# Deformable 3x3 convolution on Trainium2: sets of sampling centres with 6x10 regions, the gather over 64 rows in two partition halves, the spread in fp32, and a convolution that reads the samples in place

## The reference

```python
x1  = x + L0(gn(x))          # gn: mean and variance per image and channel; L0: 16 Fourier modes
                             # along rows and along columns, and a 1x1 mix
out = x1 + L1(gn(x1))

def L1(x):                   # deformable 3x3 convolution, 32 -> 32 channels
    om = conv2d(x, w_om, 3x3, padding 1) + b_om
    off = om[:, :18]; mask = sigmoid(om[:, 18:])
    ys = dy + ky + base_y; xs = dx + kx + base_x         # for each of the nine taps
    vals = bilinear_sample(x, ys, xs) * mask             # zero outside the image
    return einsum('bckhw,ock->bohw', vals, weight) + bias
```

## Time and profile before

| | |
|---|---|
| runs | 2192.13, 2203.97, 2210.58 us; median 2203.97 |
| span of the profiled execution | 2204.3 us |
| PE busy | 1875.0 us, 85% |
| DVE busy | 1707.6 us, 77% |
| ACT busy | 1630.4 us, 74% |
| POOL busy | 1377.4 us, 62% |
| first and last output add (L780) | 337.2 and 2197.6 us |
| DMA, data | 362.74 MB, 58.7% of 16 engines |
| DMA, instructions | 117 packets, 1.92 MB |
| chain of waits that ended last | PE 45%, DVE 16%, "issue" 13% |

### The profile page before, as it was taken

How to read it: one execution, slowest core, us unless ns; L and a number is a source line. 1 busy time by engine, 2 the same in 40 slices (tenths; PEclk the granted TensorE clock), 3 DMA queues, 4 the chain that set the end, 5 groups by cost and what they waited for, 6 DMA issues and landing times.

```text
span 2204.3 us, 126941 instructions
## 1 busy us (share of the span) xinstructions
PE 1875.0 (85%) x50241; PEld 1307.4 (59%) x50241; DVE 1707.6 (77%) x2942; ACT 1630.4 (74%) x2854; POOL 1377.4 (62%) x1803
## 2 busy tenths in 40 slices
PE   8566169988999888898999899999999999999995
PEld 3321046655666555565666666666666666666663
DVE  8689358866888667686888788888888888888883
ACT  0003358877888777787888888888888888888883
POOL 0000057766777666676777777777777777777772
PEclk9699679999999999999999999999999999999997
DMA  9026636655666555655666666666666666666663
GB/s 339 1 114 252 255 104 173 172 142 140 175 172 172 144 143 152 160 151 145 173 172 173 160 169 177 172 172 172 172 172 172 172 175 169 170 171 173 172 165 92
DMA packets 196603, 364.84 MB, mean 166 GB/s; under 512 B 39760, under 2 KB 122480, under 8 KB 192368
## 3 DMA queue, kind: packets, MB, share of 16 engines
q1 hardware_dynamic: 196464, 362.74, 58.7%
HBM read 159.38 MB, written 52.22 MB: 96 GB/s over the span
## 4 chain that ended last, share of the span: by engine, by line
PE 45%; DVE 16%; issue 13%; POOL 4%; SPq 3%; ACT 2%; DVEq 2%; DMA 1%; POOLq 0%; ACTq 0%
PE pV L987 14%; PE pE L966 10%; DVE big L753 9%; PE pM L1012 8%; PE pM L999 7%; PE pR L1026 3%; SPq L421 3%; DVE halves L748 3%; DVE big L734 3%; POOL halves L493 2%; POOL prod L484 2%; PE pM L1033 1%; ACT halves L588 1%; DVE big L761 1%; DMA v<-big 1%
## 5 line engine op out<-in xcount | busy, mean ns | idle before, releaser
L753 DVE COPY big<-pE 128x768 f32<-128x768 f32 x768 | 725.7, 945 | 256.4 <-PE pE L966 246.3
L493 POOL TENSOR_TENSOR halves<-prod,halves 128x300 f16<-128x300 f32 x768 | 604.4, 787 | 429.8 <-DVE halves L748 275.8
L594 ACT ACTIVATE big<-pE 128x768 f32<-128x768 f32 x768 | 634.5, 826 | 112.3 <-PE pE L966 111.5
L987 PE MATMUL pV<-big 128*32 128x144 f32 x16384 | 671.7, 293 | 26.5 <-issue 22.6
L484 POOL TENSOR_TENSOR prod<-big 128x300 f32<-128x300 f32 x768 | 558.7, 728 | 73.3
L966 PE MATMUL pE<-big,sel_s 32*128 32x64 f16 (+1 forms) x24576 | 412.8, 203 | 144.6 <-DVE big L753 98.9
L966 PEld LDWEIGHTS pE<-big,sel_s 32*128 32x128 f16 x24576 | 324.8, 92 | 346.8 <-issue 300.6
L987 PEld LDWEIGHTS pV<-big 128*32 128x32 f32 x16384 | 440.2, 110 | 78.1 <-issue 33.7
L734 DVE STREAM_TRANSPOSE big<-halves 128x384 f32<-128x384 f32 x768 | 439.1, 572 | 28.8 <-POOL halves L493 7.2
L608 ACT ACTIVATE big<-pV 128x432 f32<-128x432 f32 (+1 forms) x640 | 304.8, 476 | 65.2 <-PE pV L987 36.0
L1026 PE MATMUL pR<-ident,strips 128*128 128x128 f32 x2048 | 335.8, 287 | 4.4 <-issue 4.4
(11 more groups left out here) (73 smaller groups left out, 1250.4 us busy)
## 6 DMA issues: line engine op xcount, KB each, us to landing
v<-big SPq DMA_DIRECT2D x1536, 96.0 KB
win<-xh_scratch SPq DMA_DIRECT2D x128, 544.0 KB, 3.9
big<-xh_scratch SPq DMA_DIRECT2D x384, 136.0 KB, 2.6
xh_scratch<-win SPq DMA_DIRECT2D x32, 544.0 KB, 2.7
big<-in_x SPq DMA_DIRECT2D x16, 1024.0 KB, 16.7
x_scratch<-big SPq DMA_DIRECT2D x16, 1024.0 KB, 3.9
x1r<-x_scratch SPq DMA_DIRECT2D x128, 128.0 KB, 2.1
out<-outs SPq DMA_DIRECT2D x128, 128.0 KB, 1.8
```

Of the source, the lines that this page charges most:

```text
L493: nc.gpsimd.tensor_tensor(half[:, rn % 2, :, 0:SQ, 1], prod[:, rn % 2, :, :], half[:, rn % 2, :, 0:SQ, 0], ALU.subtract).then_inc(low_done, 1)
L594: nc.scalar.activation(*expanded(1 - q, r, 0), ACT.Copy).then_inc(e_act, 1)
L753: nc.vector.tensor_copy(*expanded(1 - q, r, 1)).then_inc(e_dve, 1)
L987: last = mm(pV[r % 2][b * C:(b + 1) * C, o:o + TAPC], XT[q][:, t * P + b * C:t * P + (b + 1) * C], av[:, b * NT + t, :], start=True, stop= ...
```

## The change

- **Sets in place of pairs.** The samples are made for two rows of sampling centres: a set holds, for its two rows, all taps (ky, kx) whose centre row falls on them. So the region of a tile is 6 rows instead of 8, and the tile is 4 pixels wide: `WIN_R` x `WIN_C` = 6 x 10 = 60 of 64 partitions. Two tiles lie one above the other on the partitions. An output pair needs samples of two neighbouring sets; there are 65 sets per group (`NSET`), 130 in all, for the same 128 output pairs.
- **Products and spread.** Three rounds of 600 products (`prod`, padded to 32) in place of six of 300. They stay in fp32: the casts (L748, L588) and the subtraction (L493) are gone. DVE transposes 768 elements at a time, three times. The spread is 24 fp32 matmuls per round (32 rows, 64 output columns; 128, 192 and 64 columns wide) in place of 32 fp16 ones.
- **Gather.** 16 tile positions x 4 images x 2 halves = 128 matmuls of 60 rows, 32 columns and 72 columns wide, in three groups, into both `pV` banks; before it was 64 of 128 rows and 144 wide. Each half's bank is evicted by one engine (three evictions each on DVE and ACT).
- **Convolution in place.** It reads `VS` of two sets directly: 36 matmuls (9 taps x 2 rows x 2 halves of the partitions) of 64 x 64, 128 wide, with a block-diagonal weight `wc` for two images. The 12 DMAs per pair and `v2` are gone. Output and x1 are moved in two DMAs each.
- **Banks and order.** Offsets, transposes and convolution share the banks `pMR`. The order on PE is written anew (below), six sets are in work, and offsets are computed three sets ahead. The rings of hats are four deep; ACT and POOL run four steps per iteration, PE, DVE and SP two. PE's loops have 28 iterations of two sets per group; the other 18 sets are straight code.

The diff, cut to its core:

```diff
-REG_R, REG_C = 8, 16
-TILE_R, TILE_C = 2, 8
+TILE_R, TILE_C = 2, 4
+WIN_R, WIN_C = TILE_R + 2 * REACH, TILE_C + KS - 1 + 2 * REACH
+REG = WIN_R * WIN_C
...
-ROUNDS = KS * TILE_R
-RB = IPG * KS
-RPX = RB * BLK
-RW = QUADS * RPX
-SLOT = IPG * NT
-YXM = 3 * ROUNDS // TILE_R * RB
-VGROUPS = [(0, 1, 2), (3, 4, 5), (6, 7, 8), (9, 10, 11), (12, 13), (14, 15)]
...
+ROWS = KS * TILE_R
+PB = ROWS * IPG
+ROUNDS = KS
+RPX = PB * BLK
...
+TAPC = KS * TILE_C * ROWS
+VROW = NT * KS * TILE_C
+VGROUPS = [(0, 5), (5, 10), (10, 16)]
+NG = len(VGROUPS)
+PRE = ROWS // 2
...
+MGROUPS = [(0, 2, 0), (2, 5, 1), (5, 6, 0)]
+
+KYS = ((1, 0, 2), (0, 1, 2))
...
-            peeled(-1, 4)
-            for g in range(g_count):
...
+                first, loops = g * NSET + 5, (NSET - 6) // RING * (RING // unroll)
...
+                    for u in range(unroll):
+                        step(j * unroll + (first + u), (first + u) % RING, [True] * 7,
+                             lambda n, g=g: (g, n - g * NSET))
+                peeled(first + loops * unroll, (g + 1) * NSET + 5 if g + 1 < g_count else SETS + 2)
...
-                        for ky in range(KS):
-                            sp.dma_start(v2[ky * C:(ky + 1) * C, b, :, :].rearrange("c k n -> c (k n)"),
-                                         VS[q][b * C:(b + 1) * C, ky * KS * PX:(ky + 1) * KS * PX]) \
-                                .then_inc(v2_ld, 16)
...
+                return nc.gpsimd.tensor_tensor(
+                    prod[:, buf, at:at + m, 0:SQ].rearrange("p m (a b) -> p m a b", a=NSH),
+                    hy.to_broadcast(shape), hx.to_broadcast(shape), ALU.mult)
...
-                        nc.gpsimd.tensor_tensor(half[:, rn % 2, :, 0:SQ, 1], prod[:, rn % 2, :, :],
-                                                half[:, rn % 2, :, 0:SQ, 0], ALU.subtract).then_inc(low_done, 1)
...
+                            last = nc.gpsimd.tensor_copy(
+                                strips[:, 1 - s % 2, :, h, 0:REG].rearrange("p t (r x) -> p t r x", r=WIN_R),
+                                tiles_of(1 - s % 2, h))
...
-                        nc.vector.tensor_copy(half[:, rn % 2, :, 0:SQ, 0], prod[:, rn % 2, :, :]).then_inc(high_dve, 1)
...
+                for first, end, i2 in MGROUPS:
                     for h, u in itertools.product(range(2), range(QUADS)):
+                        src = PT[part, buf, :].rearrange("p (m b t) -> p m b t", m=ROWS, b=IPG)
+                        o = pE[h * HALF:(h + 1) * HALF, u * 512:u * 512 + EPX] \
+                            .rearrange("p (m b t) -> p m b t", m=ROWS, b=IPG)
+                        last = mm(o[:, first:end], sel_s[part, i2 * KS + rn, :],
+                                  src[:, first:end, :, h * NTP:(h + 1) * NTP], start=True, stop=True)
...
-                        for t in tiles:
-                            o = (t - tiles[0]) * TAPC
-                            for b in range(IPG):
-                                last = mm(pV[r % 2][b * C:(b + 1) * C, o:o + TAPC],
-                                          XT[q][:, t * P + b * C:t * P + (b + 1) * C],
-                                          av[:, b * NT + t, :], start=True, stop=True)
...
+                for t in range(t0, t1):
+                    o = (t - t0) * TAPC
+                    for b, h in itertools.product(range(IPG), range(2)):
+                        part = slice(h * HALF, h * HALF + REG)
+                        at = (b * NTP + t) * TAPC
+                        last = mm(pV[h][b * C:(b + 1) * C, o:o + TAPC],
+                                  XT[q][part, t * P + b * C:t * P + (b + 1) * C],
+                                  A[q][part, at:at + TAPC], start=True, stop=True)
+                last.then_inc(v_done, 1)
...
+            def convolve(c, q):
...
+                for k, (ky, kx) in enumerate(itertools.product(range(KS), range(KS))):
+                    for i, r in itertools.product(range(TILE_R), range(2)):
+
+                        at = TILE_R * KYS[i].index(ky) + i
+                        own = at < PRE
+                        m = at + PRE if own else at - PRE
+                        src = VS[q if own else 1 - q].rearrange("p (m t k j) -> p m t k j", m=ROWS, t=NT, k=KS)
+                        part = slice(r * HALF, (r + 1) * HALF)
+                        last = mm(pO[i * HALF:(i + 1) * HALF, r, :].rearrange("p (t j) -> p t j", t=NT),
+                                  wc[part, k, :], src[part, m, :, kx, :], start=(k == 0), stop=(k == TAPS - 1))
+                last.then_inc(conv_done, 1)
+
+            def step(N, s, on, place):
+                q = s % 2
+                done = convolved(N - 3, place)
+                if on[0]:
+                    spread(N, 0, q)
+                if on[2]:
+                    pe.wait_ge(v_act, (N - 1) * NG)
+                    pe.wait_ge(v_dve, (N - 1) * NG)
+                    wait(pe, sub_done, min(N + 3, SETS) if isinstance(N, int) else N + 3)
+                    wait(pe, xt_done, min(N, SETS) * TCH if isinstance(N, int) else N * TCH)
+                    wait(pe, out_ready, done - 1)
+                    convolve(N - 3, 1 - q)
+                if on[1]:
+                    gather(N - 1, 1 - q, 0)
+                if on[0]:
+                    wait(pe, out_ready, done)
+                    turn_rows(N, q, 0)
+                    spread(N, 1, 1 - q)
+                    turn_rows(N, q, 1)
+                if on[3]:
+                    wait(pe, out_ready, done)
+                    offsets(N + 3, 1 - q)
+                if on[1]:
+                    gather(N - 1, 1 - q, 1)
+                if on[0]:
+                    turn_rows(N, q, 2)
+                    spread(N, 2, q)
+                if on[3]:
+                    turn_offsets(N + 3)
+                if on[0]:
+                    turn_rows(N, q, 3)
+                if on[1]:
+                    gather(N - 1, 1 - q, 2)
+            steps(pe, step, UNROLL)
```

More of the change, by code:

```diff
@@ L323, in build, with rounds @@
+        def rounds(on, N, r, ahead):
+            k, rn = divmod(r + ahead, ROUNDS)
+            return (N + k, k, rn) if on[(0, 5)[k]] else None
         block = ctx.enter_context(nc.Block())
@@ L618, in _ @@
+            steps(act, step, RING)
             act.wait_ge(flag_set, 1)
```

563 lines of the change are left out of this document (261 added, 302 removed).

## The result

| | before | changed |
|---|---|---|
| median | 2199.91 us (4 runs, 2192.13 to 2210.58) | 2773.35 us (4 runs, 2763.84 to 2777.11) |
| ratio | | 1.258, 95% interval 1.253 to 1.264 |
| span of the profiled execution | 2204.3 | 2762.0 |

What follows compares the result with a forecast made beforehand. PE was taken to be bound by instruction fetch in its loops: 330 us around the steady part, 56 iterations of 33.9 us (1898) and 18 straight sets of 13.6 (245) gave 2470 us, range 2250 to 2850.

Steps and rivals of the forecast that it cites:

- the first rival: PE's loops are kept without any instruction fetch, 12.4 us per set, 1942 us in all; chance 0.12.
- a block now holds 24.8 / 8.36 = 3.0 us of work, less than the 3.25 between restarts: PE's loops: work per instruction block is shorter than its fetch, so the fetch sets the pace, 27.2 us per iteration.
- The term for the lower clock: PE at half clock after the idle behind the closing branch: 2.3 us added per iteration.
- So 12.4 us per set: PE's time for one set with no late instruction: 10.8 us of work plus two waits of 0.8.
- 2.3 if the two partition halves run together: PE's gather per set: 128 matmuls of 72 columns, eight at once, 2.3 us; 4.6 with four at once.
- I take 3.25: Time per fetched instruction block on PE, from a late iteration's restarts before the change; fewer data packets was the reason.
- The other late return, with 3.78: Another late iteration of the kernel before, restarts 3.78 us apart; used as the slow bound, 2760 us in all.
- 4.4 behind the branch + 8.36 × 3.25 = 27.2 + 2.3 for the half clock: One iteration of PE's loops, two sets: branch idle, block fetches and lower clock, together 33.9 us.
- PE holds about 8 blocks: PE's instruction store keeps about 8 blocks; one more pushes out the loop's head. The new body is 8.36 blocks.
- Nothing is refetched: Same as the first rival: PE's store is larger than inferred or the loops are held; 1942 us, chance 0.12.
- Only four matmuls at once: PE's gather and spread take 4.6 us each instead of 2.3, 16.0 per set; 2830 us, chance 0.13.
- Only the branch stalls: Blocks come ahead of PE's work and a loop costs only its return, 29.2 us per iteration; 2188 us, chance 0.05.

Runs made afterwards that it cites:

- wide kernel: Changed kernel with the gather done in pairs of tiles, 72 matmuls per set instead of 128 over the same columns (samples partly wrong): 2001.25 us.
- straight version: Changed kernel with all 130 sets of PE's program written as straight code, no loop, other engines keeping their loops: 2444.13 us, ratio 1.133.
- The shift: Changed kernel with 29 one-column dummy matmuls (116 instructions) put once ahead of PE's straight code: 2698.31 us.
- two-group kernel: Changed kernel, loops of two sets kept, spread in two groups of 16 matmuls instead of three of 8 (one of six rows selected wrongly): 2689.76 us.
- shifted kernel before: Kernel before with 38 one-column dummy matmuls (152 instructions) put once ahead of PE's straight code: 2142.54 us, ratio 0.981.
- shifted wide kernel: The wide kernel with 32 one-column matmuls (128 instructions) once ahead of the straight code, so both loops touch 8 blocks instead of 7: 2482.59 us.

## Why the prediction was right in kind and wrong in size

**Right: the mechanism.** Every return of both loops is late; either loop fetches 10 packets per iteration, where I said 8 to 9; the branch costs 4.7 us in the second loop (4.4 forecast) and 3.6 in the first, under the 4 that I had given as the sign; the lower clock costs 2.4 in the iteration shown (spread 0.67, convolution 1.78; 2.3 forecast); the other engines don't bind. None of the three rivals is what happened. The test by itself is the wide kernel: with a body that fits, the changed kernel would be faster than before (wide 2001, with its own gather some 2105 by the estimate below), though not by as much as the 1942 of the first rival.

**Wrong: the time between two returns, and the lower clock.** The forecast said 33.9 us per iteration, and 38.9 is the mean of the two loops; 56 × 5.0 = 280 us of the 303 between forecast and result. The step that failed is "a block now holds 24.8 / 8.36 = 3.0 us of work, less than the 3.25 between restarts", so that the fetch alone sets the pace and the stretch between returns is 8.36 × 3.25 = 27.2 us. It is 30.6 on average: 24.7 of work, 0.9 of waits for DVE and ACT, and 5.0 of idle at block ends, which comes on top of the work. The term for the lower clock is 4.2 where 2.3 was forecast, and the idle behind the branch 4.1 where 4.4 was; 30.6 + 4.2 + 4.1 = 38.9.

The idles and waits are those of the two loops shown above. The 24.7 is an estimate, twice a set of the wide kernel without its waits (13.0 − 1.3, from 900 to 1000 us) plus the 0.64 of item 1, and the clock is what then remains of 41.0 and 36.8: 5.4 us in the first loop, 3.0 in the second. Term by term:

1. *"So 12.4 us per set."* The wide kernel's set takes 13.0. There a gather group of five tiles takes 0.80 us (913.37 to 914.17), in the changed kernel 1.01 to 1.02 (1546.56 to 1547.57), and the group of six 0.92 (916.71 to 917.63) against 1.14 (1009.02 to 1010.16 in the straight version). So the changed kernel's own set would take 13.0 + 0.64 = 13.65, an estimate, and a block would hold 3.3 us of it, not 3.0. The price that failed is that of the gather, "2.3 if the two partition halves run together": it takes 1.01 + 1.01 + 1.14 = 3.2. For 24 matmuls in place of 40 over the same 360 columns the time fell from 1.01 to 0.80, near the 0.72 that columns give. So with 72 columns the number of matmuls counts beside the columns: 25 ns for each in the code. Eight at once is right; four at once would be 1.4. The spread took 0.84 (1538.66 to 1539.50) and not 0.77 per round. Per iteration 2.5 us.
2. *"I take 3.25"* for a block. The pace in straight code is 3.8 to 4.0 (15.8 and 16.26 us for 4.13 blocks), so the fewer data packets on the DMA engines, my reason for the low end, didn't bring it. The other late return, with 3.78, was the better row. Straight sets took 15.8 instead of 13.6. Whether a fetch itself takes that long isn't shown: even with 4.0 us of work in a block some idle is left.
3. *"4.4 behind the branch + 8.36 × 3.25 = 27.2 + 2.3 for the half clock"* has one idle and one spell at the half clock per iteration. In the first loop there are two: the head leaves its block after 25 matmuls and waits again, and a wait of 1.9 us in the middle brings the clock down a second time. This is the difference between 41.0 and 36.8, 27 × 4.2 = 113 us in all: 2.4 us of it idle (10.3 against 7.9), the rest the clock. The shift took it out of the first loop and put 2.0 per iteration on the second.
4. *"PE holds about 8 blocks."* Not wrong for this forecast, since 9 and 10 are touched, but a loop can count on one less: the kernel before with 8 touched was late at 7 and 18 of 28 returns, the wide and two-group kernels with 8 at 51 of 54 and 27 of 27, and all six loops with 7 at none (166 returns).

Together, by runs: the changed kernel without any fetch would take 330 + 130 × 13.65 = 2105 us, an estimate from the wide kernel; running through its blocks in straight code adds 339 (2444), and the 54 late returns 329 more (2773). So the change would have gained 4% by its work (2% against the shifted kernel before), and lost 668 us to the fetch and the clock behind it. The forecast had 2473 − 1942 = 531 for these: 137 of the 300 missing are there, and 163 in the work of a set.

**The rivals.** "Nothing is refetched" (0.12): refuted by the branch rows. "Only four matmuls at once": a gather group would take 1.4, it takes 1.01. "Only the branch stalls": refuted by the straight version, which has no branch and is at 2444.

**Open.** Why a loop of 8 touched blocks is late in some iterations in one kernel and in all in another wasn't settled. The traces do show an order: by the idles in the timelines some 4 instructions of the loop lie in its eighth block where 7 of 28 returns are late, 36 where 18 of 28 are, 30 and 74 in the shifted wide kernel (24 and 27 of 27), and 194 in the two-group kernel (27 of 27). That would fit a block behind the loop that is fetched only if the branch comes late enough. The kernels with less work per block are also the ones late in nearly all, and no run tells the two apart. Nor was it shown what sets the nearly 4 us per block, or why the kernel before without loops waits for its samples. A form of the changed kernel that computes the whole reference and fits into 7 blocks wasn't found: it needs at least some 165 of PE's 1059 instructions per set fewer.

## What to carry to other kernels

Count a loop body in instructions of the engine that bounds it, fp32 matmuls as four, and in touched blocks of 256; on PE a body that touches 7 ran without any fetch, and one that touches 8 or more could pay 6 to 12 us at each return. Splitting matmuls into more and smaller ones cost twice here, in the time of each and in the length of the loop, and neither is seen in columns or busy shares. Don't take the longer of work and fetch for the time of a block where the two are near each other: here the idles came on top. If runs of one kernel scatter by some per cent, look at the longest closing branch early: shifting the loop by 152 instructions brought about 2% here.

## What the runs showed of the hardware

- The place of a loop matters as much as its length: the same work took 2001 us with bodies of 6.5 blocks on 7, and 2483 with the same bodies on 8.
- In straight code with 3.3 and 3.6 us of work in a block, blocks followed one another every 3.94 and 4.00 us on average, lower clock included. The "issue" idle per block in straight code was 0.6 us with 3.3 us of work in a block, 0.2 with 4.0 (the wide kernel between its loops) and 0.05 with some 4.5 (the kernel before without loops).
- A late iteration fetched 9 packets where 8 blocks are touched and 10 where 9 are.
- After an idle of 1.90 us (ahead of 921.21 in the changed kernel) the granted clock went to 0.51, the 1.2 GHz level, within the next microsecond, and the convolution took 3.75 instead of 2.13 us. After one of 1.97 (ahead of 1012.44 in the straight version) it stayed at 1.00, as it did after the idles of 0.8. So a two-microsecond idle can, but need not, bring the clock down.
- Matmuls of 60 x 32 with 72 columns came at 25 ns each in a row of 40, and the same columns with 24 matmuls at 33 ns each.
